# Edge pass of a graph layer on one core: a gather also waits for TensorE's message sums of the item seventeen places back

## The chip, the cores and the metric

The kernel runs on one core of one Trainium2 chip, in one launch. The metric is the time of the device in microseconds (us). Engines in the profile: PE is TensorE's matmul and PEld its weight load, DVE is VectorE, ACT is ScalarE, POOL is GpSimd, SP is SyncE. PEq, DVEq and the like are the engines' sequencers, which also do register work and issue DMAs.

## The reference, cut to what matters

6250 nodes with 256 features each, 200000 edges, sorted by their target `dst`. The change lies in the graph attention part (8 heads of 32):

```python
h = (x @ W.T).reshape(n, H, D)
h_src, h_dst = h[src], h[dst]                       # h[src]: the gathers
alpha = einsum('ehd,hd->eh', h_src, a_src) + einsum('ehd,hd->eh', h_dst, a_dst)
enc = relu(edge_attr @ edge_W.T + edge_b).reshape(-1, H, D)
alpha = alpha + sum(enc * h_dst, axis=-1)
alpha = where(alpha >= 0, alpha, 0.2 * alpha)
ex = exp(alpha - segment_max(alpha, dst)[dst])
attn = ex / maximum(segment_sum(ex, dst)[dst], 1e-10)
out = segment_sum(h_src * attn[..., None], dst).reshape(n, H * D) + bias
```

Beside it there are a linear-attention block with its feed-forward over the same nodes, ahead of the edge pass, and a routed feed-forward with 8 experts, behind it. Neither is touched.

## The kernel before, in words

The edge pass works on 440 items. An item is a stretch of 512 edges together with one tile of 125 target nodes; a stretch that touches two tiles makes two items. Item n has a position r = n mod 4 in its group of four (`G = 4`), since the running maximum over sorted edges is worked out for four items at a time.

All engines run the same list of steps k = 0, 1, 2, ..., unrolled in full, each in its own fixed order:

- **POOL** (`gather`, L514) fetches rows of `h_tab` for the sources of item n: four indirect transfers of 128 rows, 1088 bytes each, into one of 16 slots (`RING = 16`). It waits for the indices of the group (`idx_in`), for the landing of the gather six back (`gathered`, six semaphores, `NGS = 6`), and for `msg_ready` at n - 15, which says that message n - 16 has been made and the slot is free.
- **TensorE** in step k: the attention sums of item k - 2 (`e_sum`, L1061, increments `r_ready`), once a group each `g_up` (L1074 and L1075, `ends_up`), `g_down` (L1082 and L1085, `ends_down`) and `g_turn` (L1091 and L1092, `ex_turned`), then the edge encoding (`e_enc`, L1030, `enc_mm`), the target rows by a one-hot product (`e_dst`, six matmuls L1040, `d_ready`), and last the message sums of item k - 12 (`m_sum`, eight matmuls L1099, `m_used`).
- **VectorE** in step k: adds the message sums of item k - 13 into the accumulator (`m_acc`, L1549, waits for `m_used`), in one step of four after rescaling it (`g_scale`, L1532), products of item k - 1 (`e_prod`, twice L1460), parts of the group's maximum (L1473 waits for `ex_turned` and `x_kept`, L1478, L1482, L1487 waits for `ends_up`, L1494 to L1501, L1505 waits for `ends_down`, L1509 to L1514), the one-hot of item k + 1 (L1451), and last message k - 11 (`m_msg`, L1540, increments `msg_ready`), which needs the gathered rows.
- **ScalarE** in step k: the relu of the encoding (`e_relu`, L752, waits for `enc_mm`), the group's copies and exponentials (L779, L783, L790, L796), the DMAs for a later item and, where the tile changes, for a later tile (`next_tile`), the copy of the gathered source terms of item k - 1 (`keep_asrc`, L759), and the one-hot for the sums (L763, L770, L774).
- **SyncE** loads the source indices two groups ahead, once older gathers have landed (L410 to L412), and the penalties and links of a group (L420, L423).

So in VectorE's step n - 5 message n - 16 is made, which releases gather n; and TensorE's step n - 5 ends with the sums of item n - 17.

Of the kernel before, what the change touches and what calls it, by code (L numbers as in the profile page):

```python
# [51 lines left out]
RING = 16  # L52
# [20 lines left out]
def wait(eng, sem, value):  # L73

    if isinstance(value, int) and value <= 0:
        return
    eng.wait_ge(sem, value)
# [29 lines left out]
def build_program(nc, io):  # L107
    stack = ExitStack()
    with stack:
        def sem(name):  # L110
            return stack.enter_context(nc.semaphore(name))
# [40 lines left out]
        def slot(n):  # L152

            b = n % RING
            if b < RING_B:
                return gbuf[:, 4 * b:4 * b + 4, :]
            at0 = (b - RING_B) * 4 * HR
            return al[:, at0:at0 + 4 * HR].rearrange("p (c w) -> p c w", c=4)
# [148 lines left out]
        node_in = sem("node_in")  # L307
# [29 lines left out]
        dt_ready, msg_ready, oneh_ready, dist_ready, acc_added, m_used = sem("dt_ready"), sem("msg_ready"), sem("oneh_ready"), sem("dist_ready"), sem("acc_added"), sem("m_used")  # L337
# [14 lines left out]
        def item_regs(eng, which, first, count=4):  # L352

            top = [NS - 1, T - 1][which]
            return nc.values_load_multi_w_load_instructions(  # L355
                items[0:1, ds(which * ITP + first, count)], engines=[eng.engine], min_val=0, max_val=top,
                skip_runtime_bounds_check_because="the table is built within these bounds")[1]
# [116 lines left out]
        def _(pool):  # L474
# [29 lines left out]
            def gather(n):  # L504

                g = n // G
                if n % G == 0:
                    pool.wait_ge(idx_in[g % 2], 64 * (g // 2) + 64)
                wait(pool, gathered[n % NGS], 64 * (n // NGS))
                wait(pool, msg_ready, n - RING + 1)  # L510
                pool.sem_inc(went_on, 1)
                for c in range(4):
                    k = 4 * (n % G) + c
                    pool.indirect_dma_start(slot(n)[:, c, :], None, h_tab, bass.IndirectOffsetOnAxis(ap=idx[g % 2][:, k:k + 1], axis=0)).then_inc(gathered[n % NGS], 16)  # L514

            for n in range(RING_B):
                gather(n)
# [18 lines left out]
            for n in range(RING_B, RING_B + 4):  # L536
                gather(n)
            clear(r1[:, :], 0.0)
            for n in range(RING_B + 4, ITEMS):
                gather(n)  # L540
# [50 lines left out]
        def _(act):  # L591
# [147 lines left out]
            def load_tile(t):  # L739
                act.dma_start(hbt[:, ds(t & (HT - 1), 1), :, :].rearrange("p t a c -> p (t a c)"), hsplit[ds(t, 1)].rearrange("t p c -> p (t c)")).then_inc(node_in, 16)  # L740

            def next_tile(t, before):

                with act.If(t != before):
                    act.wait_ge(node_in, t * 16)
                    load_tile(t)

            def e_relu(n):
# [58 lines left out]
            for b in range(EB):  # L807
                load_item(b, s0[b])
                if b > 0:
                    next_tile(t0[b], t0[b - 1])  # L810
            act.wait_ge(wb_in, 16 * 12)
            for k in range(ITEMS + LM + 2):
                if k % EB == 0 and k < ITEMS:
                    s_next = item_regs(act, 0, k + EB - 1, EB)
                    t_next = item_regs(act, 1, k + EB - 2, EB + 1)
                if k < ITEMS:
                    e_relu(k)
                if (g := group_at(k, 5)) is not None:
                    g_x(g)
                if (g := group_at(k, 9)) is not None:  # L820
                    g_exp(g)
                if (g := group_at(k, 10)) is not None:
                    g_keep(g)
                if 0 < k < ITEMS - EB + 1:
                    b = k % EB
                    act.wait_ge(d_ready, k)
                    load_item((b - 1) % EB, s_next[b])
                    next_tile(t_next[b + 1], t_next[b])
                if 0 <= k - 1 < ITEMS:
                    keep_asrc(k - 1)  # L830
                if k % G == 0 and 8 <= k < ITEMS + 8:
                    s_dt, t_dt = item_regs(act, 0, k - 8), item_regs(act, 1, k - 8)
                if 0 <= k - 8 < ITEMS:
                    m_dt(k - 8, s_dt[k % G], t_dt[k % G])
                if 0 <= k - 10 < ITEMS:
                    m_oneh(k - 10)
                if (g := group_at(k, 12)) is not None:
                    g_fac(g)
# [46 lines left out]
        def _(pe):  # L885
# [147 lines left out]
            def e_dst(n, t):  # L1033
                q = n % 2
                pe.wait_ge(oneh_t_ready, n + 1)
                pe.wait_ge(node_in, t * 16 + 16)
                wait(pe, prod_ready, n - 1)
                for k in range(KC):
                    for a in range(3):
                        m = pe.matmul(bank[2 + 2 * q + k][:, :], hbt[:, ds(t & (HT - 1), 1), a, k * 128:(k + 1) * 128].rearrange("p t c -> p (t c)"), oneh_t[q][:, :], start=(a == 0), stop=(a == 2))  # L1040
                m.then_inc(d_ready, 1)
# [64 lines left out]
            for k in range(ITEMS + LM + 2):  # L1106
                if k % EB == 0 and k < ITEMS:
                    t = item_regs(pe, 1, k, EB)
                bank7_read(k)
                if 0 <= k - 2 < ITEMS:  # L1110
                    e_sum(k - 2)
                elif k % G == 2:
                    new_sums()
                if (g := group_at(k, 7)) is not None:
                    g_up(g)
                if k % G == 0 and 8 <= k <= G * NG + 8:
                    g_down((k - 8) // G)
                if (g := group_at(k, 10)) is not None:
                    g_turn(g)
                if k < ITEMS:  # L1120
                    e_enc(k)
                    e_dst(k, t[k % EB])
                if 0 <= k - LM - 1 < ITEMS:
                    m_sum(k - LM - 1)
# [688 lines left out]
```

## Time and profile before

| | us |
|---|---|
| median of 3 runs | 5232.41 |
| lowest and highest of the runs | 5230.8, 5269.83 |
| span of the profiled execution, first to last instruction | 5158.3 |
| TensorE matmul busy in the span | 3767.6 (73%) |
| VectorE busy | 2599.5 (50%) |
| ScalarE busy | 2112.2 (41%) |
| POOL busy | 2005.2 (39%) |
| gathers into the ring, POOL L514 | 1760 transfers, 1003 and 999 ns mean each for its two tiles |

The time of a run holds 74.1 us more than the span of the profiled execution; the profile doesn't list a time of that execution other than its span. The page puts 17% of the chain that ended last on "another core or an unknown queue", though the kernel runs on one core. The edge pass lies between about 976 us (the first message) and 4367 us (the last). Busy shares are averages over parts with different limits, so the prediction reads one part at a time.

### The profile page before, as it was taken

The numbers are of one execution on the slowest core, as the hardware profiler recorded it, in microseconds if no ns is written. First come the engines' busy times: TensorE is split into PE (matmuls) and PEld (weight loads), VectorE is DVE, ScalarE is ACT, GpSimd is POOL, SyncE is SP. The second block draws the span as 40 slices with busy tenths as digits, with TensorE's granted clock in tenths as the row PEclk, the third lists the DMA queues.
The fourth block names the chain that finished last, engine by engine and source line by source line (L and its number), as shares of the span: only waits on it lengthen the run. The fifth ranks groups of instructions, "written<-read, shape, count | busy, mean of one in ns | idle before, by whom it ended". The sixth has DMA issues, their size and how long they took to land.

```text
span 5158.3 us, 88906 instructions
## 1 busy us (share of the span) xinstructions
PE 3767.6 (73%) x22054; PEld 2527.9 (49%) x22055; DVE 2599.5 (50%) x6056; ACT 2112.2 (41%) x5703; POOL 2005.2 (39%) x2172
## 2 busy tenths in 40 slices
PE   4788997677677667677767667777766667891999
PEld 3357886344444444444434444444444444771888
DVE  5556554455555555555555555555555555440111
ACT  3212332344444444444444444444444445442332
POOL 3120000555455544455544555555554442005111
PEclk8889998788888888888888888888888888895999
DMA  4610111333333333333333333443333332102110
GB/s 151 225 44 17 34 33 49 92 99 100 97 97 101 99 99 99 97 100 100 102 100 94 101 100 99 105 102 98 102 102 100 100 101 93 72 22 59 36 36 28
DMA packets 352302, 449.27 MB, mean 87 GB/s; under 512 B 170970, under 2 KB 275163, under 8 KB 350456
## 3 DMA queue, kind: packets, MB, share of 16 engines
q0 software_dynamic: 95568, 267.78, 19.8%
q10 hardware_dynamic: 108050, 122.83, 7.8%
q1 hardware_dynamic: 148231, 53.53, 4.3%
q8 instruction: 172, 2.82, 0.2%
q14 instruction: 281, 2.30, 0.1%
HBM read 389.57 MB, written 55.13 MB: 86 GB/s over the span
## 4 chain that ended last, share of the span: by engine, by line
PE 39%; another core or an unknown queue 17%; issue 15%; DVE 12%; ACT 6%; ACTq 6%; DMA 3%; DVEq 1%; POOL 1%; SPq 0%; POOLq 0%
PE bank L1099 6%; PE bank L1040 5%; PE bank L1183 4%; PE bank L1195 4%; PE bank L1143 3%; PE bank L1005 3%; PE bank L1014 3%; ACT dist L770 3%; DVE prod L1460 3%; PE bank L1061 2%; ACTq L355 2%; DVE msg L1540 2%; ACTq L737 2%; PE bank L1030 2%
## 5 line engine op out<-in xcount | busy, mean ns | idle before, releaser
L514 POOL DMA_INDIRECT al<-h_tab,idx x976 | 975.4, 999 | 1021.5 <-issue 970.8
L752 ACT ACTIVATE enc<-bank,eb 128x512 f32<-128x512 f32 x880 | 555.3, 682 | 1601.5 <-remote 1338.1
L514 POOL DMA_INDIRECT gbuf<-h_tab,idx x784 | 786.5, 1003 | 821.3 <-issue 738.5
L1061 PE MATMUL bank<-prod,hsel 128*32 128x128 f32 x7040 | 336.9, 317 | 928.5 <-issue 779.0
L1040 PE MATMUL bank<-oneh_t,hbt 125*128 125x512 bf16 x2640 | 839.4, 464 | 38.0 <-issue 33.9
L1061 PEld LDWEIGHTS bank<-prod,hsel 128*32 128x32 f32 x7040 | 199.4, 122 | 1098.5 <-issue 916.4
L1460 DVE SCALAR_TENSOR_TENSOR prod<-enc,adst,bank 128x512 f32<-128x512 f32 x880 | 629.1, 736 | 25.8 <-remote 10.9
L1099 PE MATMUL bank<-msg,oneh 128*125 128x264 f32 x2352 | 613.1, 406 | 14.9 <-DVE r L1549 9.1
L1549 DVE TENSOR_TENSOR r<-r,bank 125x264 f32 x440 | 188.5, 428 | 757.8 <-remote 534.3
L1099 PEld LDWEIGHTS bank<-msg,oneh 128*125 128x125 f32 x2352 | 476.8, 204 | 154.4 <-issue 45.9
L770 ACT ACTIVATE dist<-iota_n,dtile 128x125 f32<-128x125 f32 x1760 | 551.1, 384 | 2.0 <-issue 0.5
L1040 PEld LDWEIGHTS bank<-oneh_t,hbt 125*128 x2640 | 258.3, 111 | 483.1 <-issue 355.5
L1099 PE MATMUL bank<-al,oneh 128*125 128x264 f32 x1168 | 319.0, 418 | 5.7 <-issue 3.4
L1099 PEld LDWEIGHTS bank<-al,oneh 128*125 128x125 f32 x1168 | 246.9, 212 | 81.7 <-issue 23.5
L774 ACT ACTIVATE oneh<-dist 128x500 f32<-128x500 f32 x440 | 272.7, 620 | 14.1 <-PE bank L1099 0.2
L1030 PE MATMUL bank<-att,ew_bf 24*128 24x512 bf16 x880 | 205.9, 453 | 58.3 <-issue 28.7
L879 ACT ACTIVATE al<-bank,b1f 128x256 f32<-128x256 f32 x224 | 106.1, 474 | 270.6 <-PE bank L1183 270.6
L523 POOL MEMSET al<- 128x2 f32 (+1 forms) x3 | 0.3, 112 | 536.2 <-DMA accd<-al 536.1
L1540 DVE TENSOR_TENSOR msg<-al 128x1056 f32<-128x1056 f32 x163 | 203.8, 1250 | 0.1
L1183 PE MATMUL bank<-al 128*128 128x256 f32 x896 | 200.7, 383 | 0.7 <-ACT al L873 0.7
L1014 PE MATMUL bank<-r 128*125 128x256 f32 x800 | 200.2, 379 | 0.0
L1005 PE MATMUL bank<-r 128*128 128x250 f32 x800 | 198.6, 377 | 0.0
(255 smaller groups left out, 5399.6 us busy)
## 6 DMA issues: line engine op xcount, KB each, us to landing
dstb<-dst ACTq DMA_DIRECT2D x440, 125.0 KB
al<-pen_d SPq DMA_DIRECT2D x1760, 4.0 KB
att<-attrx ACTq DMA_DIRECT2D x880, 24.0 KB
al<-h_tab,idx POOLq DMA_INDIRECT x976
link<-links SPq DMA_DIRECT2D x880, 0.2 KB
gbuf<-h_tab,idx POOLq DMA_INDIRECT x784
attrx<-al ACTq DMA_DIRECT2D x8, 1176.0 KB, 12.3
hsplit<-hb POOLq DMA_DIRECT2D x25, 375.0 KB, 5.2
```

The source lines that it names most:

```text
L514: pool.indirect_dma_start(slot(n)[:, c, :], None, h_tab, bass.IndirectOffsetOnAxis(ap=idx[g % 2][:, k:k + 1], axis=0)).then_inc(gathered[n ...
L752: m = act.activation(enc[n % 2][:, k, :], bank[k][:, :], ACT.Relu, bias=eb[:, k:k + 1])
L770: m = act.activation(dist[q][:, c, :], iota_n[:, :], ACT.Abs, bias=dtile[n % NDT][:, c:c + 1], scale=-1.0)
L1005: m = pe.matmul(bank[FB3[j % 4]][:, 0:W2T], w1m[:, k, j * 128:(j + 1) * 128], ynT[:, k, :], start=(k == 0), stop=(k == KC - 1))
L1014: m = pe.matmul(bank[3 + u][0:P, 0:C], f1[:, j, u * P:(u + 1) * P], w2m[:, j, :], start=(j == 0), stop=(j == JF - 1))
L1030: m = pe.matmul(bank[k][:, :], ew_bf[32 * k:32 * k + 24, k * 128:(k + 1) * 128], att[b][32 * k:32 * k + 24, :], start=True, stop=True)
L1040: m = pe.matmul(bank[2 + 2 * q + k][:, :], hbt[:, ds(t & (HT - 1), 1), a, k * 128:(k + 1) * 128].rearrange("p t c -> p (t c)"), oneh_t[q][ ...
L1061: m = pe.matmul(bank[7][32 * c:32 * c + 32, 0:128], hsel[:, i, :], prod[n % 2][:, k, c * 128:(c + 1) * 128], start=(i == 0 and k == 0), st ...
L1099: m = pe.matmul(bank[6][0:P, 0:HO], oneh[n % NM][:, c, :], msg[n % NM][:, c, :], start=(c == 0), stop=(c == 3))
L1183: m = pe.matmul(bank[FB[j % 4]][:, 0:256], w1f[:, k, j * 128:(j + 1) * 128], xdT[:, k, :], start=(k == 0), stop=(k == KC - 1))
L1460: m = v.scalar_tensor_tensor(prod[q][:, k, :], enc[q][:, k, :], adst[:, k:k + 1], bank[2 + 2 * q + k][:, :], ALU.add, ALU.mult)
L1540: v.tensor_tensor(msg[n % NM][:, :, :].rearrange("p c (h e) -> p c h e", h=H), slot(n)[:, :, 8:HR].rearrange("p c (h e) -> p c h e", h=H), ...
```

## The change

One wait is added in `gather`. With `RING = 16` it asks `m_used` for n - 16, which holds once TensorE has posted the sums of items 0 to n - 17; for n up to 16 it asks for nothing. In two other places the tile number t, which is at most 49, is masked with 63 before it is multiplied into the value that a semaphore is compared with.

```diff
@@ gather(n), POOL
                 wait(pool, gathered[n % NGS], 64 * (n // NGS))
                 wait(pool, msg_ready, n - RING + 1)
+                wait(pool, m_used, n - RING)
                 pool.sem_inc(went_on, 1)
@@ next_tile(t, before), ScalarE
                 with act.If(t != before):
-                    act.wait_ge(node_in, t * 16)
+                    act.wait_ge(node_in, (t & 63) * 16)
                     load_tile(t)
@@ e_dst(n, t), TensorE
                 pe.wait_ge(oneh_t_ready, n + 1)
-                pe.wait_ge(node_in, t * 16 + 16)
+                pe.wait_ge(node_in, (t & 63) * 16 + 16)
                 wait(pe, prod_ready, n - 1)
```

## Rows read from the trace of the kernel before

**Rows 1.** Busy time by stretch: length, then each engine's busy us, clock, DMA, GB/s.

```profile
1000.00:4300.00 3300.00, 2316.10 (x14894) 1372.31 (x14883) 1797.00 (x3667) 1528.06 (x4293) 1681.73 (x1680) 0.83 0.39 100
2503.62:2535.97 32.35, 20.28 (x142) 12.20 (x141) 17.11 (x36) 14.44 (x42) 15.39 (x16) 0.83 0.38 100
...
4304.87:4329.31 24.44, 21.24 (x144) 12.90 (x143) 17.50 (x36) 14.81 (x44) 4.04 (x4) 0.86 0.17 43
```

**Rows 2.** Waits, 1000 to 4300 us: waiting line and its releaser, total us, times, longest.

```profile
DVE r L1549 <- remote: 519.1, 77, 9.7
DVE carry L1505 <- remote: 259.3, 62, 5.8
DVE al L1473 <- remote: 123.1, 37, 5.3
...
ACT enc L752 <- remote: 1295.1, 235, 12.3
```

**Rows 3.** Order of time, 2515 to 2536 us: start, length, instruction, idle before it.

```profile
2515.11 0.16 DVE L1505 COPY carry<-bank 128x2 f32<-128x2 f32 x1 [5.43 <-remote]
...
2516.82 1.25 DVE L1540 TENSOR_TENSOR al<-gbuf,al 128x1056 f32<-128x1056 f32 x1
...
2518.85 0.95 POOL L514 DMA_INDIRECT gbuf<-h_tab,idx  x1 [5.26 <-issue]
...
2525.15 1.95 PE L1099 MATMUL bank<-al,oneh 128*125 128x264 f32 x8
2525.30 0.94 POOL L514 DMA_INDIRECT gbuf<-h_tab,idx  x1 [1.75 <-issue]
...
2527.25 0.43 DVE L1549 TENSOR_TENSOR r<-r,bank 125x264 f32 x1 [2.73 <-issue]
...
2527.62 0.49 PE L1092 MATMUL bank<-ident,al 128*128 128x128 f32 x2
...
2528.04 0.39 PE L1030 MATMUL bank<-att,ew_bf 24*128 24x512 bf16 x2
2528.36 1.47 PE L1040 MATMUL bank<-oneh_t,hbt 125*128 125x512 bf16 x6
...
2529.66 1.95 PE L1099 MATMUL bank<-msg,oneh 128*125 128x264 f32 x8
...
2531.52 0.29 DVE L1473 SCALAR_TENSOR_TENSOR al<-al 128x128 f32<-128x128 f32 x1 [3.84 <-remote]
...
2535.97 0.94 POOL L514 DMA_INDIRECT al<-h_tab,idx  x1 [5.98 <-issue]
```

**Rows 4.** The same view of another cycle, 2709 to 2727 us.

```profile
2709.38 0.94 POOL L514 DMA_INDIRECT al<-h_tab,idx  x1 [5.21 <-issue]
...
2715.25 0.94 POOL L514 DMA_INDIRECT al<-h_tab,idx  x1 [1.13 <-issue]
2715.49 2.14 PE L1099 MATMUL bank<-al,oneh 128*125 128x264 f32 x8
...
2718.16 0.51 PE L1092 MATMUL bank<-ident,al 128*128 128x128 f32 x2
...
2721.22 0.37 PE L1030 MATMUL bank<-att,ew_bf 24*128 24x512 bf16 x1 [1.05 <-issue]
2721.53 0.43 DVE L1549 TENSOR_TENSOR r<-r,bank 125x264 f32 x1 [7.05 <-remote]
...
2721.87 0.28 DVE L1473 SCALAR_TENSOR_TENSOR al<-al 128x128 f32<-128x128 f32 x1
...
2726.31 0.94 POOL L514 DMA_INDIRECT al<-h_tab,idx  x1 [6.37 <-issue]
...
2726.62 0.43 DVE L1549 TENSOR_TENSOR r<-r,bank 125x264 f32 x1 [1.08 <-PE bank L1099]
```

**Rows 5.** The same view, 2507 to 2509 us, at a gather with r = 0.

```profile
2507.94 0.43 DVE L1549 TENSOR_TENSOR r<-r,bank 125x264 f32 x1 [0.18 <-issue]
...
2508.89 0.94 POOL L514 DMA_INDIRECT gbuf<-h_tab,idx  x1 [0.30 <-issue]
```

## The prediction

> **What bounds the kernel now.** I read the busy shares by stretch first. The edge pass takes most of the span, at 1000 to 4300 us no engine is busy for more than 70% of it (TensorE 2316 of 3300 us), and the DMA engines for 39%. Its work repeats every four items: one such cycle takes 32.35 us, and the cycle near the end, when nearly all gathers have been issued, takes 24.44 us for the same compute instructions [rows 1]. So some 7 us of a cycle go with the gathers, though VectorE hardly ever waits for gathered rows.
>
> Then the waits, to see for what it does wait. VectorE's accumulate L1549 waited 519.1 us in 77 waits for a "remote" releaser; the carry L1505 259.3 us, the leaky step L1473 123.1 us; ScalarE's L752 1295.1 us [rows 2]. All four wait on semaphores that TensorE increments, on this one core. "Remote" is only what the profile writes when it finds no releaser close by.
>
> Then the order of time. In [rows 3] TensorE's L1092 ends at 2528.11 and L1099 at 2531.61, while VectorE's L1473, which needs L1092, starts at 2531.52, 3.4 us late. In [rows 4] L1099 ends at 2717.63, and the L1549 that needs it starts at 2721.53; L1092 ends at 2718.67, and L1473 starts at 2721.87. A gather's four transfers were issued at 2525.30 and 2715.25 on. Both times TensorE's news comes out 6.2 to 6.6 us after the first issue, several items at once. I read it so: while gather traffic runs, TensorE's increments are held, and they come out together as the item's traffic ends; an increment that comes up to some 2 us after the first issue can still pass, as in [rows 3], where L1099 ends 1.80 us after it and L1549 follows at 2527.25. In [rows 4] one at 2.38 us did not pass: there the item before had been issued only 5.87 us earlier (2709.38), so its traffic had not ended. TensorE itself slows too: L1030 starts at 2721.22 only, with 1.05 us idle ahead of it.
>
> **The change part by part.** The item is n = 4g + r. Its gather is released now by message n - 16, and starts 0.78 us after that message ends (2516.82 + 1.25 = 2518.07; the issue is at 2518.85) [rows 3], unless POOL is still issuing. It will also need TensorE's sums of item n - 17, posted.
>
> 1. r = 0. The sums were already posted when VectorE began L1549 at 2507.94, 0.95 us ahead of the issue at 2508.89, which POOL's own issuing sets [rows 5]. The cost is nothing; the cover is POOL's back-to-back issue.
>
> 2. r = 1. The gather at 2518.85 needs sums that TensorE ran one step back; what was held then came out when L1505 was let go, at 2515.11 [rows 3], 3.7 us ahead of the issue. Nothing.
>
> 3. r = 2. Here the wait binds in every cycle. Message n - 16 ends before TensorE has finished the sums: L1099 ends at 2527.10 against an issue at 2525.30, and at 2717.63 against 2715.25 [rows 3, 4]. With 0.78 us from release to issue, the gather starts at 2527.9 and 2718.4, so 2.6 and 3.2 us later. In return the increments that come next find an open door: L1092 at 2528.11 and 2718.67 is 0.2 us after the first issue. L1473 then starts 3.3 us (2531.52 to 2528.2) and 3.1 us earlier, and in [rows 4] L1549 3.8 us earlier.
>
> 4. r = 3. This takes most of it back. The sums that this gather needs are the next L1099. In [rows 3] it ends at 2531.61, 3.7 us after the new issue and so inside the traffic: it is held until 6.2 us after the issue, 2534.1. The gather goes at 2534.9 instead of 2535.97: 1.1 us earlier. In [rows 4] TensorE would no longer idle before L1030, so its L1099 ends some 3.5 us after L1092 as in [rows 3] (2528.11 to 2531.61), at 2722.2, is held until 2718.4 + 6.3 = 2724.7, and the gather goes at 2725.5 instead of 2726.31; VectorE's L1549 starts at 2724.8 instead of 2726.62, so the next step is 0.8 to 1.8 us ahead. From there the cycle runs as before. The lead of 3 us that VectorE and ScalarE had won is spent waiting for this post: what is late next is L1549 of the step after.
>
> 5. Nobody starves. A gather is issued six items ahead of its first use (L759) and 16 ahead of its message, at 8 us an item; 3 us less lead stays covered. SP, which waits for landed gathers, loads indices two groups of four ahead and links a group and a half ahead, so 3 us are covered there too. If that cover were gone, a cycle would pay up to the whole 3 us.
>
> 6. One more semaphore on POOL's sequencer: it falls in the 0.78 us of the items where POOL waits, or behind its issuing. POOL does several register operations in the 0.30 us between two issues [rows 5], so I estimate one check at under 0.1 us: 212 items with r = 2 or 3, at most 21 us. A gain is excluded, since an instruction is added. I take nothing.
>
> 7. t & 63 leaves every t (0 to 49) as it is. On ScalarE it stands in a branch taken 49 times. On TensorE it is one more register operation for each of 440 items, ahead of L1040. That starts at 2528.36, before L1030's end at 2528.43 [rows 3], so L1030's 0.39 us cover it: nothing. Without the cover, at under 0.1 us by the same estimate, 44 us.
>
> The sum: 1.1 us in a cycle as in [rows 3], 0.8 to 1.8 us in one as in [rows 4]; I take 1.0 us, since some cycles have long issues that I can't place. The ring is full from item 17 on: 423 items, 106 cycles, 106 us. The span goes from 5158.3 to about 5052. The runs' median of 5232.41 is 74.1 us above the span, which stays; 5232 - 106 = **5126 us**. The ends: nothing gained in a cycle (the held time is 7 us instead of 6.2), and 2.5 us gained (below).
>
> The Trainium skill speaks against this change: "DMA: Bandwidth & Descriptors", section Rules for kernel authors, says to issue a DMA early, do compute, and wait on its semaphore late. By that rule a gather that is issued 3 us later can win nothing and may cost. The rows disagree as far as VectorE's waits go: they are on TensorE, not on gathers.
>
> **The rivals.**
>
> A, slower: the hold is longer than I take it. Now the r = 2 traffic holds back little of the last part of TensorE's step; moved 3 us later it lies right over the increments of L1040 (ending at 2529.83) and L1099 (2531.61), which VectorE's next step and the r = 3 gather both need. The gather r = 3 follows its predecessor by hold + 0.8 us, and today it follows by 10.67 us (2525.30 to 2535.97), of which 2.6 to 3.2 us are now spent ahead. So a hold of more than about 7.2 us turns the sign. For it: such long waits occur. Against: the holds in both quoted cycles are 6.2 to 6.6 us. The longest wait of L1549 is 9.7 us against 7.05 in [rows 4]; were that 2.65 us more of hold, 8.9 us, a cycle would lose 1.7 us: 106 x 1.7 = 180 us, 5412 us.
>
> B, no change that can be told: the hold is near 7 us, or the gain of a cycle ends in the stall of the carry L1505 (259.3 us in 62 waits [rows 2]), which hangs on where the r = 0 and r = 3 traffic lies and which this change doesn't address. 0 to 0.5 us a cycle: 5180 to 5232 us. That the new wait is always met already would give the same, but L1549's 77 waits of 6.7 us speak against it.
>
> C, more: the r = 3 sums slip out ahead of or between the transfers. Then the gather needs only message n - 16, which is 3.3 us earlier, and POOL's four issues (5.3 us after 2527.9): it goes at 2533.2, 2.5 us or more earlier, 106 x 2.5 = 265 us, 4967 us. For it: some cycles' increments do pass late. Against: L1099 ends 3.7 us into the traffic, later than any that I saw pass.
>
> **How the numbers follow.** The forecast gets 0.50, A 0.15, B 0.22, C 0.13. A measurement of this kernel can tell about 1% from no change, 5180 to 5285 us. The forecast's own range is 5060 to 5190 us. For 8 in 10 I take in B, half of C and the mild part of A: **4985 to 5265 us**. Faster by over 1%: nearly all of the forecast and C, 0.60; within 1%: B, the forecast's upper edge and a mild A, 0.26; slower 0.14.
>
> **What would show it.** POOL: the gather r = 2 follows r = 1 by 8.5 to 9.5 us (now 5.87 to 6.45), r = 3 follows r = 2 by 7 to 7.5 us (now 10.67 to 11.06); their sum falls by 1. VectorE: the long waits of L1549 at r = 2 become 2.7 to 4 us, L1473's vanish, and a new wait of L1549 of some 2 us stands one step later. L1505's waits stay. A cycle with gathers takes 30.5 us. I am wrong if the r = 2 gather isn't later (the wait never bound), if L1473 still waits 3 us (the door is not what I think), or if L1505's waits change by more than a fifth.

## The result and the profile after

The changed kernel takes 5005.81 us (median of 4 runs, 4985.47 to 5021.78) against 5247.18 us for the kernel before (median of 4, 5230.8 to 5269.83): a ratio of 0.9537, 95% interval 0.9498 to 0.9576. It is faster by 4.6%; the forecast was 2%.

The profiled execution of the changed kernel took 5021.78 us with a span of 5019.9. So only 1.9 us lie around a span. The 74.1 us between the span of 5158.3 and the listed median, then, were not work around the span: the profiled execution of before took some 5160 us (5158.3 + 1.9, an estimate), less than any of the four runs of before. The difference of the medians, 241.4 us, is 138.4 us between the two profiled spans, 87.0 us by which before's median lies above its profiled execution (5247.2 - 5160.2), and 16.0 us by which after's lies below (5021.8 - 5005.8). Whatever is taken from the two traces side by side therefore shows less than the whole gain.

Busy time by stretch of the changed kernel, in the columns of [rows 1]: the edge pass, and one cycle of four items.

```profile
1000.00:4300.00 3300.00, 2416.15 (x15411) 1439.04 (x15410) 1869.46 (x3826) 1585.15 (x4456) 1790.73 (x1692) 0.84 0.40 104
2374.00:2403.00 29.00, 24.62 (x149) 13.82 (x147) 17.64 (x37) 16.44 (x47) 16.72 (x16) 0.84 0.42 108
```

The same 3300 us hold 4% more VectorE work than in [rows 1] (1869.46 against 1797.00 us): every engine gets its work sooner. The pass, from the first message to the last accumulate, fell from 3394.6 to 3256.6 us, which is all but 0.4 us of the change of the span. A cycle of four, averaged over the accumulates of items 19 to 419, fell from 31.56 to 30.11 us. The line numbers after the new line are one higher: L1099 is L1100, L1473 is L1474, L1505 is L1506, L1549 is L1550.

The waits from 1000 to 4300 us, in the columns of [rows 2]:

```profile
ACT enc L753 <- remote: 1212.7, 236, 9.3
DVE r L1550 <- remote: 263.5, 72, 6.2
DVE r L1550 <- PE bank L1100: 255.2, 100, 4.8
DVE al L1474 <- remote: 230.0, 36, 8.3
...
DVE carry L1506 <- remote: 163.2, 34, 7.0
DVE edge L1488 <- remote: 159.5, 37, 7.4
POOL gbuf L515 <- PE bank L1100: 133.6, 39, 6.2
POOL al L515 <- PE bank L1100: 125.1, 37, 6.5
```

Of the copy of the group's ends, L1488 here, the same view of before has:

```profile
DVE edge L1487 <- remote: 35.6, 30, 3.3
```

The accumulate's remote waits halved (519.1 to 263.5 us). The last two rows of the view of after are the new wait: POOL's gathers held up 76 times by TensorE's sums in some 110 cycles. A further 67 waits of POOL (137.2 us) are put down to "remote"; before has none. The carry's waits fell (259.3 to 163.2 us), but those of the leaky step grew (123.1 to 230.0), and so did those of L1488 (35.6 to 159.5). VectorE's remote waits on all four went from 937.1 us to 816.2.

Two cycles of the changed kernel in order of time. In the first, the r = 2 gather goes out at 2389.64; in the second, at 2539.43.

```profile
2385.19 1.25 DVE L1541 TENSOR_TENSOR msg<-al 128x1056 f32<-128x1056 f32 x1
...
2386.81 1.95 PE L1100 MATMUL bank<-al,oneh 128*125 128x264 f32 x8
...
2388.91 0.43 DVE L1550 TENSOR_TENSOR r<-r,bank 125x264 f32 x1 [2.47 <-PE bank L1100]
...
2389.28 0.49 PE L1093 MATMUL bank<-ident,al 128*128 128x128 f32 x2
2389.64 0.95 POOL L515 DMA_INDIRECT al<-h_tab,idx  x1 [4.14 <-PE bank L1100]
...
2389.88 0.29 DVE L1474 SCALAR_TENSOR_TENSOR al<-al 128x128 f32<-128x128 f32 x1 [0.54 <-PE bank L1093]
...
2391.32 1.95 PE L1100 MATMUL bank<-msg,oneh 128*125 128x264 f32 x8
...
2392.23 2.14 POOL L515 DMA_INDIRECT al<-h_tab,idx  x1 [0.30 <-issue]
...
2393.51 0.43 DVE L1550 TENSOR_TENSOR r<-r,bank 125x264 f32 x1
...
2395.93 1.10 POOL L515 DMA_INDIRECT al<-h_tab,idx  x1 [0.30 <-issue]
...
2539.43 0.95 POOL L515 DMA_INDIRECT al<-h_tab,idx  x1 [2.42 <-issue]
...
2539.75 0.49 PE L1093 MATMUL bank<-ident,al 128*128 128x128 f32 x2
...
2545.55 0.29 DVE L1474 SCALAR_TENSOR_TENSOR al<-al 128x128 f32<-128x128 f32 x1 [6.74 <-remote]
```

The first cycle shows how the change can pay. By its message alone the gather would have gone out at some 2387.2 (2386.44 and the 0.78 us from release to issue); it is 2.4 us later. VectorE's L1474 follows TensorE's L1093 at once, and TensorE's next sums, which end at 2393.27, 3.6 us into the traffic, reach VectorE at 2393.51 all the same. They end within an issue that took 2.14 us in place of 0.95. The r = 3 gather starts 6.29 us after that of r = 2, where [rows 3] has 10.67. The second cycle is the other kind: L1093 ends 0.81 us after the first issue, and its increment is seen 6.1 us after that issue.

### The profile page after: what moved, and what is told of

Same layout as the page of the kernel before. It is cut to its first block, busy times and chain, and to the rows that moved or that the text cites. A ratio compares the mean times of both kernels' runs of the same rounds, so it can differ in the third digit from the quotient of the medians.

```text
span 5019.9 us, 89713 instructions
## 1 busy us (share of the span) xinstructions
PE 3767.7 (75%) x22054; PEld 2525.2 (50%) x22055; DVE 2605.4 (52%) x6056; ACT 2110.6 (42%) x5703; POOL 2107.5 (42%) x2172
## 4 chain that ended last, share of the span: by engine, by line
PE 48%; another core or an unknown queue 16%; issue 13%; DVE 11%; ACT 4%; ACTq 4%; DMA 3%; POOL 1%; DVEq 1%; SPq 0%; POOLq 0%
PE bank L1100 9%; PE bank L1041 8%; PE bank L1184 4%; PE bank L1196 4%; PE bank L1144 4%; PE bank L1006 3%; PE bank L1015 3%; PE bank L1062 3%; DVE prod L1461 3%; PE bank L1031 2%; ACT dist L771 2%; DVE msg L1541 2%; PE bank L919 1%; PE bank L1065 1%
## 5 line engine op out<-in xcount | busy, mean ns | idle before, releaser
L515 POOL DMA_INDIRECT al<-h_tab,idx x976 | 1022.7, 1048 | 794.9 <-issue 298.5
L515 POOL DMA_INDIRECT gbuf<-h_tab,idx x784 | 840.5, 1072 | 808.8 <-issue 383.8
L1062 PE MATMUL bank<-prod,hsel 128*32 128x128 f32 x7040 | 325.6, 309 | 763.0 <-issue 505.1
L1100 PE MATMUL bank<-msg,oneh 128*125 128x264 f32 x2352 | 628.5, 413 | 26.9 <-DVE r L1550 18.0
L1100 PEld LDWEIGHTS bank<-msg,oneh 128*125 128x125 f32 x2352 | 488.1, 208 | 173.0 <-issue 61.1
L1550 DVE TENSOR_TENSOR r<-r,bank 125x264 f32 x440 | 188.2, 428 | 559.4 <-remote 263.5
L1100 PE MATMUL bank<-al,oneh 128*125 128x264 f32 x1168 | 314.0, 413 | 10.9 <-DVE r L1550 7.2
L1100 PEld LDWEIGHTS bank<-al,oneh 128*125 128x125 f32 x1168 | 241.5, 208 | 90.1 <-issue 34.3
L1541 DVE TENSOR_TENSOR msg<-al 128x1056 f32<-128x1056 f32 x163 | 203.8, 1250 | 0.1
```

The source lines that it names most:

```text
L1062: m = pe.matmul(bank[7][32 * c:32 * c + 32, 0:128], hsel[:, i, :], prod[n % 2][:, k, c * 128:(c + 1) * 128], start=(i == 0 and k == 0), st ...
L1100: m = pe.matmul(bank[6][0:P, 0:HO], oneh[n % NM][:, c, :], msg[n % NM][:, c, :], start=(c == 0), stop=(c == 3))
L1541: v.tensor_tensor(msg[n % NM][:, :, :].rearrange("p c (h e) -> p c h e", h=H), slot(n)[:, :, 8:HR].rearrange("p c (h e) -> p c h e", h=H), ...
```

## The experiments

All are edits of the changed kernel, which holds the masks of the node waits; line numbers differ by a few. They ran in batches, each on one chip, with the kernel before beside them. There turned out to be two kinds of chip. On three (0, 12 and 15, as the runs number them) the kernel before takes 4192 to 4199 us, and no wait of VectorE, ScalarE or POOL in the edge pass is put down to "remote". On two (3 and 10) it takes 5176 to 5247 us, with such waits, as in the traces of before and after. I call the first free and the second holding; what makes a chip the one or the other stays open. The level can differ between batches on one chip too: chip 3 has 5247 us in one and 5176 in another. Ratios are only taken within a batch.

**On a free chip: the parts, and the whole.**

The masks alone:

```diff
-                wait(pool, m_used, n - RING)
```

> The masks of the tile number without the new wait. If the gain (ratio 0.954) comes from the wait, as both the theory of held increments and the theory of mere pacing say, this is the kernel before: 0.99 to 1.01. If the masks change how the waits on the tile loads are built and that is what helps, 0.95 to 0.97. A cost of the added register operations on TensorE would show as up to 1.01.

4199.21 against 4198.44 us, ratio 0.9999 (0.998 to 1.0019).

The wait at one residue only:

```diff
-                wait(pool, m_used, n - RING)
+                if n % G == 2:
+                    wait(pool, m_used, n - RING)
```

> The new wait on one gather of four only, the one with r = 2 (masks in). The theory of held increments, as my prediction has it, puts the whole of the binding there: 0.95 to 0.97, near the full change. If the gain comes from spacing all gathers out (pacing), a quarter to a half of it: 0.975 to 0.99.

4198.83 us, ratio 1.0009 (0.9993 to 1.0025). With `== 3` in place of `== 2`:

> The new wait on the gather with r = 3 only (masks in). Without the delay at r = 2 TensorE's sums are posted before that gather's message nearly always (VectorE's next accumulate hardly waits there), so the wait doesn't bind: 0.99 to 1.01 by the theory of held increments. By pacing some gain, 0.98 to 0.99.

4195.28 us, ratio 0.9987 (0.9971 to 1.0004). With the sums of one item later:

```diff
+                wait(pool, m_used, n - RING + 1)
```

> The wait one item stronger: the gather also needs TensorE's sums of the item sixteen places back, which TensorE makes one step later. Each gather then starts behind TensorE's step n - 4 instead of n - 5, and never beside the step's increments; gathers never run back to back. By held increments the hold then covers the start of each TensorE step only: 0.93 to 0.97 if the serial chain of gather (6.2 us hold and 0.8 us issue) is shorter than the cycle, 4 x 7.1 = 28.4 us against 30.1 us of the change. If the gather chain becomes the bound, slower than the change: 0.97 to 1.05.

4209.32 us, ratio 1.0031 (1.0011 to 1.005). The whole change:

> The whole change once more, on a chip on which the kernel before may take some 5240 us (with waits of DVE, ACT and POOL put down to 'remote') or some 4198 us (without them). Theory T (the change pays only where TensorE's semaphore increments come out late while gather traffic runs): ratio 0.945 to 0.965 if the kernel before takes 5230 us or more in this run, and 0.998 to 1.004 if it takes some 4200 us. Rival P (the change merely paces the gathers, and pays whatever else happens): 0.95 to 0.97 on either. Rival N (the slow kernel before was an exception, and the change is worth nothing of itself): within 0.5% on either.

4196.98 against 4192.07 us, ratio 1.0005 (0.9986 to 1.0025). Its busy time by stretch on this chip (12):

```profile
1000.00:3500.00 2500.00, 2138.24 (x15265) 1335.08 (x15254) 1830.48 (x3784) 1574.13 (x4391) 1808.65 (x1666) 0.93 0.54 135
```

and the same kernel's on chip 3 (its run stands below):

```profile
1000.00:3500.00 2500.00, 1841.08 (x11804) 1086.27 (x11802) 1426.89 (x2908) 1208.56 (x3404) 1406.99 (x1334) 0.84 0.41 104
```

One program, and 28% more VectorE work done in the same 2500 us on the free chip. TensorE is busy for 86% of it and bounds the pass; the page's chain of the mask-only run gives it 79% of the span. So the change is worth nothing where increments come out at once. Rival P, that pacing the gathers pays by itself, is out. The masks do nothing here either, nor, in the run without the wait at r = 2 below, on a holding chip. The expectations for the first four runs were made for a holding chip and are not decided by these runs. The wait at r = 2 alone was measured on a holding chip as well (below); the masks alone, the wait at r = 3 alone and the wait for the sums of one item later were not, so whether a stronger tie would pay more there stays open.

**On holding chips: is it a delay, or the tie to TensorE?** Thirteen chained memsets of two numbers stand ahead of the r = 2 gathers in place of the wait:

```diff
-                wait(pool, m_used, n - RING)
+                if n % G == 2:
+                    for _i in range(13):
+                        pool.wait_ge(paced, 13 * g + _i)
+                        pool.memset(pace[:, :], 0.0).then_inc(paced, 1)
```

> The kernel before (with the two node waits of the change), and ahead of the gather of every item n with n mod 4 = 2 GpSimd does 13 chained memsets of two numbers, some 2 to 3 us, in place of the new wait. Rival P (any later issue of that gather pays): where the kernel before takes 5230 us or more, 4950 to 5130 us, cycle of four about 30 us. Theory T (what pays is that the gather is tied to TensorE's posted sums, so that posts made meanwhile find no transfers under way): less than a third of the change's 240 us, so 5160 us or more. On a chip on which the kernel before takes some 4200 us neither speaks: within 0.5% of it, with GpSimd's idle time per cycle (5.0 us in the mask-only run) covering the memsets.

Chip 10: 5283.64 against 5227.79 us, one run each. That is too few for the 1.1% to count, but far from the gain that rival P wanted. The r = 2 gather follows that of r = 1 by 7.92 us (8.28 in the changed kernel, 6.16 before), the r = 3 gather follows by 9.70 us, against 7.61, and a cycle takes 32.78 us. A delay of this length doesn't pay. It isn't the same delay, though: in 63 of 102 cycles the gather still starts before TensorE's sums have ended (0.27 us before at the median), where in the changed kernel it always starts at least 0.8 us behind them. In the 39 cycles in which it starts behind them, the r = 3 gather follows by 8.36 us, in the other 63 by 10.53. The rows point to where the gather lies against TensorE's sums as what counts; a longer fixed delay, which would lie behind them too, was not run.

**Which of the four waits.**

> The whole change once more, beside its parts, so that they can be compared on one chip. Where the kernel before takes 5230 us or more: ratio 0.945 to 0.965 by every theory. Where it takes some 4200 us: 0.998 to 1.003, as before.

> The new wait kept for the gathers of items n with n mod 4 = 2 alone, where the prediction says that it binds. Where the kernel before takes 5230 us or more: the prediction's theory (binding at r = 2 alone makes the gain) wants the whole gain, ratio within 0.01 of the full change's; rival Q (after the change all four gathers wait, and the others' waits are what lets the r = 3 sums out at once) wants at least half of the gain to be missing, ratio 0.975 or more. Where the kernel before takes some 4200 us: within 0.3% of it.

The complement has `if n % G != 2:` in the same place.

> The complement: the new wait at the gathers of items n with n mod 4 = 0, 1 and 3, and none at 2. Where the kernel before takes 5230 us or more: the prediction's theory wants no gain, ratio 0.99 to 1.01, with the spacing from the gather of r = 1 to that of r = 2 at 5.9 to 6.5 us as before the change; rival Q wants half of the gain or more, ratio 0.975 or less. Where the kernel before takes some 4200 us: within 0.3% of it.

Chip 3, the kernel before at 5247.47 us: the whole change 5000.16, ratio 0.9517 (0.946 to 0.9574); r = 2 alone 5188.59, ratio 0.9886 (0.9842 to 0.9931); all but r = 2 5250.14, ratio 1.001 (0.9977 to 1.0044). Neither theory had this. The wait at r = 2 alone brings a quarter of the gain (1.14 of 4.83%), the other three bring nothing, and together they bring all of it.

The gathers' mean spacings (us, from POOL's rows, items 20 to 429) show where the rest went. The row of before is from the execution of some 5160 us, 1.7% under this batch's median of before; the other three rows are of this batch, and all but r = 2 has the median of before in it (its profiled execution took 5274.5 us, and its wait at r = 3 binds in half of the cycles, by some 0.8 us):

| | r0 to r1 | r1 to r2 | r2 to r3 | r3 to r0 |
|---|---|---|---|---|
| before | 8.04 | 6.16 | 11.21 | 6.11 |
| whole change (chip 3) | 7.28 | 8.20 | 7.47 | 6.99 |
| r = 2 alone | 9.90 | 8.14 | 7.35 | 6.25 |
| all but r = 2 | 9.52 | 5.96 | 11.62 | 5.37 |

Within the batch, against all but r = 2, the wait at r = 2 alone pays 2.2 us ahead of the r = 2 gather and wins 4.3 us behind it, but behind r = 0 it stays at 9.90 us, where the whole change has 7.28. One cycle of it, in order of time:

```profile
2456.72 1.10 POOL L516 DMA_INDIRECT al<-h_tab,idx  x1 [0.30 <-issue]
2456.75 1.95 PE L1101 MATMUL bank<-msg,oneh 128*125 128x264 f32 x8
...
2460.65 0.95 POOL L516 DMA_INDIRECT al<-h_tab,idx  x1 [0.30 <-issue]
...
2461.91 0.94 POOL L516 DMA_INDIRECT al<-h_tab,idx  x1 [0.30 <-issue]
...
2465.67 0.95 POOL L516 DMA_INDIRECT al<-h_tab,idx  x1 [0.30 <-issue]
...
2468.73 0.43 DVE L1551 TENSOR_TENSOR r<-r,bank 125x264 f32 x1 [9.28 <-remote]
2468.88 0.69 ACT L754 ACTIVATE enc<-bank,eb 128x512 f32<-128x512 f32 x1 [8.15 <-remote]
...
2474.12 0.95 POOL L516 DMA_INDIRECT al<-h_tab,idx  x1 [7.51 <-issue]
```

The r = 3 gather goes out from 2456.72 on, and that of r = 0 right behind it at 2461.91, because its message had been made by 2459.45. Eight transfers run without a pause, and twelve with those of r = 2, from 2450.43 on. TensorE's sums ended at 2458.70; VectorE got them at 2468.73, and the r = 1 gather came 12.2 us after that of r = 0. Gathers of r = 0 that follow within 6 us of r = 3 are 77% with r = 2 alone and 30% with the whole change. They are no new thing: the trace of before has 63%, all but r = 2 has 97%. Behind such a pair the r = 1 gather comes 9.1 us later in before and 10.9 us with r = 2 alone, otherwise 6.2 and 6.6 us. That led to the next pair.

```diff
-                wait(pool, m_used, n - RING)
+                if n % 2 == 0:
+                    wait(pool, m_used, n - RING)
```

> The new wait at the gathers of items n with n mod 4 = 0 and 2. On a chip on which the kernel before takes 5150 us or more: theory S (the waits at r = 2 and r = 0 make the gain together: the one lets the sums of r = 3 out at once, the other keeps the gather of r = 1 from being late in turn) wants the full change's ratio of 0.95 within 0.01, and the spacing from r = 0 to r = 1 back from 9.9 to some 7.3 us. The rival (it is the waits at 1 and 3 that count, though they bind in 1 to 7 of 100 cycles) wants 0.98 to 0.99, as with r = 2 alone. Where the kernel before takes some 4200 us: within 0.3% of it.

This fell on a free chip: 4190.52 against 4197.22 us, ratio 0.9986 (0.9963 to 1.0009). Once more:

> The new wait at the gathers of items n with n mod 4 = 0 and 2, once more. Where the kernel before takes 5150 us or more: theory S (the two waits make the gain together) wants the full change's ratio, 0.94 to 0.96, and some 7.3 us from the gather of r = 0 to that of r = 1; the rival (the waits at 1 and 3 count) wants 0.98 to 0.99. Where it takes some 4200 us: within 0.3% of it.

Chip 10: 4923.73 against 5180.7 us, ratio 0.951 (0.9445 to 0.9575). Theory S held: the two waits are the whole change. (The wait at r = 0 by itself was not run. In all but r = 2 it is there, but it holds POOL up in 3 of 100 cycles only, since POOL is still issuing r = 3.) The spacing from r = 0 to r = 1 is 6.96 us, a cycle 29.5 us. As it costs nothing on a free chip and has half of the waits, it is as good as the change, and no measurement here tells it from it.

**Is it the gathers that hold the increments?** One of an item's four transfers is left (the first 16 items keep all four), and the wait values follow:

```diff
-                for c in range(4):
+                for c in range(4 if n < RING else 1):
```

> The kernel before (with the masked node waits), with one of an item's four gather transfers only, from item 16 on; three quarters of the rows are left as they were in the buffer. Theory T (increments are late only while gather transfers run) wants, where the kernel before takes 5150 us or more, a time near that of a chip without late increments, 4150 to 4400 us, and at most a quarter of the waits put down to 'remote'. The rival that such a chip delays TensorE's increments whatever runs wants 5000 us or more. Where the kernel before takes some 4200 us: 4170 to 4200 us, as TensorE bounds it there.

Free chip: 4185.06 against 4197.22 us, ratio 0.9972 (0.9957 to 0.9987). Once more:

> The kernel before with one of an item's four gather transfers only, from item 16 on (the rest of the rows are left as they were), once more. Where the kernel before takes 5150 us or more: theory T (increments are late only while gather transfers run) wants 4150 to 4400 us and at most a quarter of the waits put down to 'remote'; the rival that such a chip delays TensorE's increments whatever runs wants 5000 us or more. Where the kernel before takes some 4200 us: 4185 us, as measured before.

Chip 10: 4222.06 against 5180.7 us, ratio 0.8146 (0.8111 to 0.818). The same chip, without three quarters of the gather transfers, is within 0.9% of a free one (4185.06 us for this kernel). Waits and busy time by stretch (1000 to 4100 and to 3500 us), then a few rows in order of time:

```profile
ACT enc L756 <- PE bank L1034: 465.6, 335, 2.5
...
DVE r L1553 <- PE bank L1103: 236.8, 113, 3.9
...
1000.00:3500.00 2500.00, 2138.58 (x15330) 1330.20 (x15329) 1843.88 (x3801) 1587.53 (x4442) 399.66 (x427) 0.93 0.26 67
```

```profile
2501.36 0.94 POOL L518 DMA_INDIRECT al<-h_tab,idx  x1 [4.30 <-DVE msg L1544]
2501.52 0.43 DVE L1553 TENSOR_TENSOR r<-r,bank 125x264 f32 x1 [0.93 <-PE bank L1103]
2501.89 0.49 PE L1096 MATMUL bank<-ident,al 128*128 128x128 f32 x2
...
2502.89 0.69 ACT L756 ACTIVATE enc<-bank,eb 128x512 f32<-128x512 f32 x1 [0.57 <-PE bank L1034]
2502.93 0.29 DVE L1477 SCALAR_TENSOR_TENSOR al<-al 128x128 f32<-128x128 f32 x1 [0.98 <-PE bank L1096]
```

Not one wait of the edge pass is "remote" any more. The leaky step's input (L1096, the L1092 of before) ends at 2502.38, 1.0 us after the issue of a transfer, and VectorE has it 0.55 us later. Of the increments of `m_used` all 440 have a record, and of those for items 30 to 419 one of 390 comes more than 0.02 us after the sums end, though 12 of them end within 0.5 us after the issue of a transfer: one transfer by itself holds nothing up. That the gathers, at four transfers an item, cause the late increments is shown; it was only argued in the prediction.

**What of the gathers?** Two kinds of kernel were to split this further, and fell on free chips.

```diff
-                    pool.indirect_dma_start(slot(n)[:, c, :], None, h_tab, ...)
+                    pool.dma_start(slot(n)[:, c, :], h_tab[128 * k:128 * k + 128, :])
```

> The kernel before (with the masked node waits), with each indirect gather of 128 rows replaced by a plain transfer of 128 rows that lie together, same bytes and size, issued by GpSimd at the same place. The rows are others than the sources', so what is summed differs. Where the kernel before takes 5150 us or more: if GpSimd's software queue is what holds the increments, some 5000 to 5300 us; if it is the working out of the indirect addresses (the 0.95 us during which GpSimd is busy for each), 4150 to 4500 us. Where it takes some 4200 us: 4170 to 4210 us.

4198.75 against 4197.22 us, ratio 1.0007 (0.9993 to 1.0021).

> The kernel before (with the masked node waits), with each indirect gather of 128 rows replaced by a plain transfer of 128 rows that lie together, issued by GpSimd at the same place; what is summed differs. Where the kernel before takes 5150 us or more: if transfers on GpSimd's software queue hold the increments whatever their form, 4900 to 5300 us; if it is the indirect form (its 0.95 us of GpSimd's work for each, or rows scattered over memory), 4150 to 4500 us. Where it takes some 4200 us: 4199 us, as measured before.

4191.69 against 4199.26 us, ratio 0.9991 (0.9967 to 1.0016), on another free chip. The edit below moves the transfers to SyncE's program, ahead of each group's items and behind its links:

```diff
+            def load_rows(n):
+                wait(sp, gathered[n % NGS], 64 * (n // NGS))
+                wait(sp, msg_ready, n - RING + 1)
+                for c in range(4):
+                    k = 4 * (n % G) + c
+                    sp.dma_start(slot(n)[:, c, :], h_tab[128 * k:128 * k + 128, :]).then_inc(gathered[n % NGS], 16)
...
                 load_links(g - 2)
+                if g < NG:
+                    for n in range(G * g, G * g + G):
+                        load_rows(n)
```

> The kernel before (with the masked node waits), with GpSimd's gathers taken out and plain transfers of the same bytes (128 rows that lie together, four for each item) issued from SyncE's hardware queue in their place; what is summed differs. Where the kernel before takes 5150 us or more: if bytes on their way into SBUF hold the increments, 5000 us or more; if it is GpSimd's software queue or its work, 4150 to 4450 us and no waits put down to 'remote'. Where it takes some 4200 us: 4170 to 4250 us.

4494.93 against 4197.22 us, ratio 1.0719 (1.0694 to 1.0745): slower for a reason of its own, and outside what I expected. VectorE's scan waited 300.2 us in 88 waits for the links, whose transfers now queue behind SyncE's waits for messages. None of these runs says what in the gathers holds the increments: bytes, queue, or POOL's work on the addresses stay open.

**Fewer, longer stretches.** If pauses between gathers are what counts, fewer and longer ones might do more:

```diff
-                wait(pool, msg_ready, n - RING + 1)
-                wait(pool, m_used, n - RING)
+                if n % 2 == 0:
+                    wait(pool, msg_ready, n - RING + 2)
+                    wait(pool, m_used, n - RING + 1)
```

> From the changed kernel: the gathers of two items go out together (eight transfers), at even items, when the message two places further than before has been made and the sums of the item before that are posted (n - RING + 2 and n - RING + 1 in place of n - RING + 1 and n - RING); odd items wait for neither. Where the kernel before takes 5150 us or more: by theory T increments wait for a pause in the transfers, and two pauses of about 4 us each in a cycle of four in place of four short ones may go either way: under 4900 us if the pauses are what counts (ratio under 0.945), over 5050 us if the length of one stretch (8 transfers, some 10 us) is, since TensorE's chain from encoding to message sums then stands still for that long. Where it takes some 4200 us: within 0.5% of it.

Free chip: 4211.16 against 4199.26 us, ratio 1.0021 (1.0003 to 1.0038).

> The gathers of two items together at even items, as in the pairs run before, once more. Where the kernel before takes 5150 us or more: under 4900 us if the number of pauses in the gather traffic is what counts (a ratio under 0.945, better than the change), over 5050 us if the length of one stretch of transfers is; in between, a ratio of 0.945 to 0.975, neither decides. Where it takes some 4200 us: 1.000 to 1.004, as measured before.

Chip 3: 5500.28 against 5176.4 us, ratio 1.0618 (1.0574 to 1.0661). The end of one pair of gathers, in order of time:

```profile
2500.05 1.47 PE L1042 MATMUL bank<-oneh_t,hbt 125*128 125x512 bf16 x6
...
2501.36 1.95 PE L1101 MATMUL bank<-al,oneh 128*125 128x264 f32 x8
...
2504.01 0.94 POOL L516 DMA_INDIRECT al<-h_tab,idx  x1 [0.30 <-issue]
2506.38 0.16 DVE L1507 COPY carry<-bank 128x2 f32<-128x2 f32 x1 [5.32 <-remote]
2506.42 0.69 ACT L754 ACTIVATE enc<-bank,eb 128x512 f32<-128x512 f32 x1 [7.21 <-remote]
...
2511.69 1.08 PE L1063 MATMUL bank<-prod,hsel 128*32 128x128 f32 x16 [8.38 <-issue]
```

ScalarE, VectorE and then TensorE all stand until 1.4 us after the last issue has ended (2504.95 to 2506.38). TensorE is idle for 8.38 us. The length of one stretch counts: the step from encoding to sums crosses between engines several times, and little crosses meanwhile. It is also what r = 2 alone left standing: its gathers of r = 3 and r = 0 form such a pair in 77% of the cycles.

## Why the prediction was right, and where it failed

**What held.** TensorE's increments come out late while gathers run, and the tie to TensorE lets some of them out. The new wait binds at r = 2 (in 89% of cycles the gather starts some 0.86 us after a posting of the sums). The gather of r = 2 moved from 6.16 to 8.28 us after that of r = 1 (forecast 8.5 to 9.5), that of r = 3 from 11.21 to 7.61 us after r = 2 (forecast 7 to 7.5). Step 2 (nothing at r = 1) held: that wait can be left out. Step 5, nobody starves, and step 7, the masks, held: the run on a free chip puts the masks at 0.8 us of 4198, within its uncertainty. No part that costs anything was found in step 6 either. The time of 5005.81 us lies in the wide range (4985 to 5265), but 54 us below the forecast's own (5060 to 5190), between the forecast and rival C.

**The size was off by more than two: 1.0 us a cycle was forecast, 2.3 us were found.** 241.4 us over 106 cycles are 2.3 us, and chip 3 again has 247 us. The two traces alone would say 1.45 us (31.56 to 30.11), since that of before is of an execution faster than its runs. The sentence "the runs' median is 74.1 us above the span, which stays" was wrong (after has 1.9 us there), and in a kernel of one core nothing that the profile shows lies around a span for 74 us, which could have warned me. But the gain doesn't hang on that level: with r = 0 and r = 2 it is 257 us on chip 10, where before takes 5181. The missing 1.3 us a cycle are in the steps.

**Step 1 (r = 0: "The cost is nothing") is the step that failed most.** On chip 3 the wait at r = 2 alone, for which the sum had 106 us, brought 59 us (5247.47 to 5188.59). The whole change brought 247, and the waits at r = 0 and r = 2 make all of it (0.951 on chip 10). So some 188 us hang on the wait at r = 0, which the sum put at nothing from one row [rows 5]. For the cycle of before that row is typical: in 89% of the r = 0 gathers VectorE has the sums by 0.3 us before the issue. With r = 2 alone they reach VectorE only after it in 61%, 6.0 us after at the median, since the sums can now end in the traffic of r = 3 and r = 0, as in the cycle above. The prediction costed each wait in the cycle of before, not in the one that the first wait makes. And the cover that it named, POOL's back-to-back issue, is itself a stall: behind an r = 0 gather that follows r = 3 at once the next gather is 3 us later (9.1 against 6.2 us in before). The wait at r = 0 breaks up these pairs, from 77% of the cycles with r = 2 alone to 30%. Rival B had the carry's stall hang on "where the r = 0 and r = 3 traffic lies", and held that the change doesn't address it; it does.

**Step 4 (r = 3 takes most of it back) failed in nearly half of the cycles.** It held the r = 3 sums until 6.2 us after the issue. In the changed kernel 42 of 93 such sums that ended within the r = 2 gather's traffic reached VectorE within 0.6 us. All 42 ended in a gather of which one issue took over 1.5 us, like the one of 2.14 us above (22 others in such a gather didn't pass); of the 29 in a gather without a long issue, none passed. It is the long issue itself that matters: of the 48 sums that ended while it lasted, 41 passed. Long issues were in the trace of before (15% of the items have one, 38% in the changed kernel), and the prediction set them aside as "long issues that I can't place". This is rival C's mechanism (chance 0.13), by another way than it named: a pause in POOL's own issuing. Why an issue is long, and why more are in the changed kernel, isn't settled; a free chip has them too (44% of the items in the mask-only run).

**The signs.** Of the three things that I said would prove me wrong, the first didn't come (the r = 2 gather is later), the second did (the leaky step still waits, 230.0 us), and so did the third (the carry's waits fell by 37%). The door closes sooner than I read: [rows 3] shows an increment passing 1.80 us after the first issue, and the second cycle above one that was held at 0.81 us. The gathers cost more than "some 7 us" a cycle: with a quarter of the transfers a cycle takes 22.7 us against 31.6. Rival A, the only slower one, needed holds of over 7.2 us as the rule. Long ones exist (a wait of 8.3 us at most for the leaky step), but the pass is faster; only with pairs of gathers does such a kernel get slower. Rival B is what a free chip shows. The rule that spoke against the change (the Trainium skill, "DMA: Bandwidth & Descriptors", Rules for kernel authors: issue a DMA early, wait late) does not decide it: the gathers are still issued many items ahead of their use, and to issue them some 2 us later costs nothing on a free chip (1.0005) and wins on holding ones (0.9517).

## What to carry to other kernels

A wait that an engine doesn't need can pay if what it delays was standing in the way of others; find what the waiting engines wait for, then what runs at those moments, and test it by taking that away (here three of four transfers); a delay says little unless the trace shows that it moved the work to the right place. When a wait is added, go through the cycle again with it in place before calling the other places free: here most of the gain hangs on the wait at r = 0, which binds only once there is one at r = 2. And before a forecast sets a span against a median, see whether both can be of the same kind of execution; a gain that depends on the chip has to be measured on both kinds.

## What the runs showed of the hardware that I had not expected

- The same kernel takes 4192 to 4199 us on three chips and 5176 to 5247 us on two. The difference is not compute speed: VectorE's and ScalarE's instructions take the same time on both (736 ns for L1460, 1250 and 1248 ns for L1540's messages), as do most gather issues (946 ns at the median of both). It is in increments of TensorE. In the mask-only run on chip 12 the increment of `m_used` is recorded 14 to 15 ns after its matmuls end, from the 5th to the 99th of 100. In the trace of before only 340 of the 440 increments have a record of their own; these lie 0.4 us at the median, and one in four over 3.8 us, behind the last sums that ended ahead of them, and the holds are longer than that where several come out at once.
- One transfer for an item in place of four removes this almost altogether (0.8146 on a holding chip). Eight in a row make it worse (1.0618).
- Increments get out during an issue of POOL that takes 1.5 to 2.15 us in place of 0.95: 41 of 48 in the changed kernel, among the r = 3 sums that end in one.
- TensorE's mean granted clock goes with it: 0.83 in the pass of before, and 0.93 where no wait is put down to "remote", on a holding chip with a quarter of the gathers as on a free one.
